# Quartered first chunk, reordered first tile, and the V tiles moved behind the QK tiles in a differential-attention and ternary-MLP kernel

## The chip, the cores and the metric

The kernel runs on one NeuronCore of a Trainium2 chip (trn2). The metric is the time of one execution on the device in microseconds (us). Engines: PE is TensorE (matrix products and transposes), DVE is VectorE, ACT is ScalarE, POOL is GpSimd, SP is SyncE, which issues nearly all the DMAs. "SPq" and "ACTq" in rows are DMA issues by SP and ACT.

## The reference, cut to what matters

One pre-norm transformer layer on `x` of shape (8, 1024, 512), float32. The head of the kernel, which the change edits, computes the normalised rows and their products with `w_qkv`.

```python
h = layernorm(x)                          # eps 1e-5, no weight
qkv = h @ w_qkv                           # (8, 1024, 1536)
q, k, v = split(qkv, 3)                   # 16 heads of 32; each head in halves of 16
a = softmax(q1 @ k1.T * s) - lam * softmax(q2 @ k2.T * s)
out = rms_norm(a @ v) * norm_w * 0.2      # then heads folded back into rows
x = x + fold(out) @ wo
h = layernorm(x)
r = relu(bitlinear(h, w_fc) + gate * (h @ v_.T @ fast_b.T @ u.T))
x = x + bitlinear(r * r, w_proj)          # ternary weights, hidden 2048
```

Products are made at near float32 accuracy from a high and a low part of both operands: `hi*hi + hi_x*lo_w + lo_x*hi_w`.

## The kernel before

**Chunks.** The 8192 rows of x are 16 chunks of 512 rows (two for each of the 8 batches, C = 0 to 15). A chunk is loaded into `xin` (128 partitions, 4 quarters `st` of 128 rows, 512 columns), normalised in place, turned by 16 PE transposes of 128x128 and split into `xhi(C)` (ACT) and `xlo(C)` (DVE).

**Tiles.** From a chunk, 12 tiles of 512 columns follow, each of 12 matmuls (4 parts `k` of the inner dimension, 3 products `part`). Indices 0 to 7 are query and key tiles (called QK tiles below) and 8 to 11 are value tiles (V tiles). `ORDER` says in which order they come; `kind_of(T)` gives chunk and index of tile T, and chunk 0 uses `ORDER[0]`, chunk 1 `ORDER[2]`. For a QK tile ACT copies PSUM to a staging slot, DVE makes the low half and the row maximum (`dve_low`, `dve_bound`), and SP stores it to DRAM as two DMAs of 256 KB. For a V tile ACT alone copies it into `vsg[V % 2]` (two slots; V = 7 goes to `stg`), and SP stores it as one DMA. ACT waits before V >= 2 until the store of V - 2 has landed (`act_tile`).

**The prologue.** 24 tiles (T = 0 to 23) of batch 0 are made ahead of the attention, in PSUM banks T % 4. Interleaved at fixed places are the LayerNorm of the next chunk (`dve_ln_step`, steps 0 to 3 statistics, 4 gather, 6 Newton, 7 to 10 apply), its turns (after tiles 6 to 9 of chunk 0, 5 to 8 of chunk 1: `FIRST_TURN`), ternary weights of the MLP (`UNIT_AT`, ACT and DVE), and the "flag" for the largest score (`dve_flag`, `pe_flag`, then `sync_shift`, four small DMAs from `mh` that ACT issues). SP goes through one fixed list: the stores in the order of T, the loads of x chunks behind T = 10 and T = 22, the loads of queries and keys for the first head pair behind T = 15, of its values behind T = 16 and at the end.

**Into the attention.** `pe_score(e, 0, 0, 0)` is the first score. It waits for the shift DMAs of `sync_shift` and for `s_ql >= 16` and `s_v >= 8`, that is for ACT to have copied the last V tile. From there 64 head pairs run, each with 3 more tiles of later chunks, then the MLP.

**The first chunk before.** One DMA of 1 MB loads it; DVE does the whole LayerNorm; then `pe_turn` turns it by column parts `k` (four transposes each, over all quarters), ACT copies the four parts after its four weight copies `wqh`, and DVE alternates `wql` part k and `xlo` part k. Tile 0 follows k by k, three products at a time, each k waiting for its `wql` and its `xlo`.

Of the kernel before, what the change touches and what calls it, by code (L numbers as in the profile page):

```python
# [33 lines left out]

TILE_BANK = (6, 7, 6)
ORDER = ((0, 1, 8, 2, 3, 9, 4, 5, 10, 6, 7, 11), (0, 1, 8, 2, 3, 9, 4, 5, 6, 7, 10, 11),
         (0, 1, 8, 2, 3, 4, 5, 6, 7, 9, 10, 11))

STG = 8

# [61 lines left out]
def build(nc, x, wqkv, wo, lq1, lq2, lk1, lk2, norm_w, fast_b, w_fc, w_proj, u, v, gate, out):  # L102
# [10 lines left out]
    with ExitStack() as top:  # L113
# [146 lines left out]
        sb2 = (sb2a, sb2b)  # L260


        s_small, s_x, s_wo, s_xr, s_x2 = (sem(n) for n in ("s_small", "s_x", "s_wo", "s_xr", "s_x2"))
        s_nw = sem("s_nw")
        s_w = [sem(f"s_w{k}") for k in range(4)]
# [213 lines left out]
                .then_inc(s_pap, 1)  # L479

        def sync_x(e, C):
            if C:
                e.wait_ge(s_xt, 4 * C)
            e.dma_start(xin[:], x_chunk(C)).then_inc(s_x, 16)

        def sync_part(e, P):

# [185 lines left out]
            e.dma_start(out_rows[rows:rows + 128, :], fo[:, rt, :]).then_inc(s_out[rt], 16)  # L673

        def sync_program(e):
            sync_x(e, 0)
            for k in range(4):
                e.dma_start(wst[:, k, :], wqk[:, k, :]).then_inc(s_w[k], 16)
            e.dma_start(gatec, gate.partition_broadcast(128)).then_inc(s_small, 16)
# [80 lines left out]
        def pe_turn(e, C, k, bk):  # L760
# [2 lines left out]
                t = e.transpose(ps[:, bk, st * 128:(st + 1) * 128], xin[:, st, k * 128:(k + 1) * 128], ident[:])  # L763
            t.then_inc(s_xt, 1)

        def pe_part(e, P):

            C, st = part_of(P)
            e.wait_ge(s_pap, P + 1)
            e.wait_ge(s_pt, 2 * P + 1)  # L770
            for k in range(4):
                t = e.transpose(ps[:, 4, k * 128:(k + 1) * 128], xin[:, st, k * 128:(k + 1) * 128], ident[:])  # L772
            t.then_inc(s_xt, 1)
# [9 lines left out]
        def pe_tile(e, T, bk, n0, n1):  # L783

            C, i = kind_of(T)
            if n0 == 0 and T == 2:
                e.wait_ge(s_wl, 8)
            for n in range(n0, n1):
                k, part = divmod(n, 3)
                if T == 0 and part == 0:  # L790
                    e.wait_ge(s_wl, k + 1)
                if i == 0 and part == 0 and C < 3:
                    e.wait_ge(s_xtl, 4 * C + k + 1)
                elif i == 0 and n == 0:
                    e.wait_ge(s_xtl, 4 * C + 4)
                w = (wqh, wql, wqh)[part]
                xx = (xhi(C), xhi(C), xlo(C))[part]
                if i < 8:
                    m0 = TILES[i] * 128
                    t = e.matmul(ps[:, bk, :], w[:, k, m0:m0 + 128], xx[:, k, :], start=(n == 0), stop=(n == 11))  # L800
                else:
                    st = i - 8
                    t = e.matmul(ps[:, bk, :], xx[:, k, st * 128:(st + 1) * 128], w[:, k, 2 * E:3 * E],  # L803
                                 start=(n == 0), stop=(n == 11))
            if n1 == 12:
                t.then_inc(s_tile, 1)
# [284 lines left out]

        def tensor_program(e):
            e.wait_ge(s_pool, 7)
            for k in range(4):
                pe_turn(e, 0, k, k)
            for T in range(24):
                C, i = divmod(T, 12)
                if T >= 4:
                    tile_read(e, T - 4)
                else:  # L1100
                    e.wait_ge(s_xtl, T + 1)

                if T == 21:
                    pe_tile(e, T, T % 4, 0, 10)
                    pe_flag(e, 0)
                    pe_tile(e, T, T % 4, 10, 12)
                else:
                    pe_tile(e, T, T % 4, 0, 12)
                k = i - FIRST_TURN[C]
                if 0 <= k < 4:  # L1110
                    if C:
                        e.wait_ge(s_xtl, 4 * C + k + 1)
                    pe_turn(e, C + 1, k, 4 + k)
# [109 lines left out]
        def act_turn(e, C, k, bk):  # L1223
            e.wait_ge(s_xt, 4 * C + k + 1)
            if C >= 2 and k == 0:
                e.wait_ge(s_tile, 12 * (C - 1))
            e.activation(xhi(C)[:, k, :], ps[:, bk, :], ACT.Copy).then_inc(s_xth, 1)

        def act_part_ln(e, w):
            e.wait_ge(s_pnv, 8 * w + 5)  # L1230
# [154 lines left out]
        def scalar_program(e):  # L1385
            e.preload_act_table_set("natural_log_exp_and_others")
            e.wait_ge(s_pool, 4)
            act_ln(e, 0, mv, ln_t, rs)
            for k in range(4):
                e.wait_ge(s_w[k], 16)  # L1390
                e.activation(wqh[:, k, :], wst[:, k, :], ACT.Copy).then_inc(s_wh, 1)
            for k in range(4):
                act_turn(e, 0, k, k)
            for T in range(24):
                C, i = divmod(T, 12)
                act_tile(e, T, T % 4)
                if T == 3:
                    e.wait_ge(s_lamv, 4)
                    e.activation(dt_[:, 2:4], dt_[:, 0:2], ACT.Exp).then_inc(s_lame, 1)
                if i == FIRST_TURN[C] - 2:  # L1400
                    act_ln(e, C + 1, mv, ln_t, rs)
                k = i - FIRST_TURN[C]
                if 0 <= k < 4:
                    act_turn(e, C + 1, k, 4 + k)
                if T == 21:

                    sync_shift(e, 0)
                if T in UNIT_AT:
                    act_magnitudes(e, UNIT_AT.index(T))
                if T - 2 in UNIT_AT:  # L1410
                    act_ternary(e, UNIT_AT.index(T - 2))
                if T == 22:
                    e.wait_ge(s_wo, 16)
                    for r in range(2):
                        e.wait_ge(s_tna[r], 16)
                    e.activation(woh[:], wos, ACT.Copy).then_inc(s_woh, 1)
# [102 lines left out]
        def dve_ln_step(e, C, n):  # L1519
# [1 line left out]
            att, f = C < 3, C - 1  # L1521
            xi, xo = (xin, xin) if att else (x2[(f + 1) % 3], xn)
            st_, mv_, ln_, rs_ = (st6, mv, ln_t, rs) if att else (st62, mv2, ln2, rs2)
            if n == 0:
                if att:
                    e.wait_ge(s_x, 16 * (C + 1))
                else:
                    e.wait_ge(s_x2l[(f + 1) % 3], 16 * (f // 3 + 1))
            if n < 4:
# [10 lines left out]
        def dve_turn(e, C, k, bk):  # L1540
            e.wait_ge(s_xth, 4 * C + k + 1)
            e.tensor_tensor(xlo(C)[:, k, :], ps[:, bk, :], xhi(C)[:, k, :], ALU.subtract).then_inc(s_xtl, 1)  # L1542

        def dve_part_stats(e, P):

            C, st = P // 4 + 3, P % 4
            for n in range(P - 1, P) if P else range(-4, 0):

                if n < 0:
                    e.wait_ge(s_x, 16 * 4)  # L1550
                else:
                    e.wait_ge(s_xp[n % 4], 16 * (n // 4 + 1))
                e.bn_stats(st6[:, n % 4, :], xin[:, n % 4, :]).then_inc(s_pst, 1)
# [209 lines left out]
        def vector_program(e):  # L1763
# [7 lines left out]
            for k in range(4):  # L1771
                e.wait_ge(s_wh, k + 1)
                e.tensor_tensor(wql[:, k, 0:2 * E], wst[:, k, 0:2 * E], wqh[:, k, 0:2 * E], ALU.subtract).then_inc(s_wl, 1)
                dve_turn(e, 0, k, k)
            for k in range(4):
                e.tensor_tensor(wql[:, k, 2 * E:3 * E], wst[:, k, 2 * E:3 * E], wqh[:, k, 2 * E:3 * E], ALU.subtract) \
                    .then_inc(s_wl, 1)
            for T in range(24):
# [16 lines left out]
                    e.wait_ge(s_nw, 16 * 4)  # L1795
                    e.tensor_scalar(nw[:], nw[:], 1.0 - LAMBDA_INIT, None, ALU.mult).then_inc(s_lamv, 1)
                k = i - FIRST_TURN[C]
                for n in ((0, 1, 2), (3, 4), range(6, 11))[k + 3] if -3 <= k < 0 else ():
                    dve_ln_step(e, C + 1, n)
                if T - 1 in UNIT_AT:  # L1800
                    dve_ternary(e, UNIT_AT.index(T - 1))
                if T == 20:
                    dve_flag(e, 0, 0)
                if 0 <= k < 4:
                    dve_turn(e, C + 1, k, 4 + k)
                if T == 21:
                    dve_flag(e, 0, 1)
                    flag = load_flag(e, 0)
                    dve_shift(e, flag, 0)
# [165 lines left out]
```

## Time and profile before

| what | value |
|---|---|
| time before, median of 3 runs | 3751.72 us (3751.03 to 3753.09) |
| the profiled execution | 3749.25 us, its span 3747.5 us |
| PE busy | 3704.4 us, 99% of the span |
| DVE / ACT / POOL busy | 84% / 75% / 17% of the span |
| first matmul of tile 0 / first score | 16.61 us / 100.83 us |
| mean granted TensorE clock | 0.998 |

The span runs from the first to the last instruction; the execution's own time is 1.75 us longer. Times in rows are us from the span's start. A timeline row gives start, duration of the whole group, engine, line, operation, output<-inputs, count and, in brackets, idle time before it and what ended it.

### The profile page before, as it was taken

To read this page: it belongs to the slowest core of one execution; us is meant where nothing else is said; L and a number is where in the kernel's file an instruction comes from. 1 tells how busy PE (TensorE), PEld (TensorE's weight loads), DVE (VectorE), ACT (ScalarE), POOL (GpSimd) and SP (SyncE) were. 2 spreads that over 40 slices of the span, in tenths; PEclk is the share of its full clock that TensorE was granted. 3 is DMA by queue.
4 is the path that set the end of the run, shared out by engine and by line. 5 is a ranking of instruction groups with operands and counts; after the bars stand their busy time and mean duration, and the time that the engine had idled before them with its cause. 6 is when DMAs were issued, how large, how long until landed. Compare 5 with 4: busy or idle time off the path is not lost.

```text
span 3747.5 us, 57714 instructions
## 1 busy us (share of the span) xinstructions
PE 3704.4 (99%) x21736; PEld 2051.2 (55%) x21736; DVE 3153.3 (84%) x2918; ACT 2795.3 (75%) x3626; POOL 622.9 (17%) x281
## 2 busy tenths in 40 slices
PE   7999999999999999999999999999999999999999
PEld 6344444444444444444444444444468888888887
DVE  6899999999999999999999999988875555555554
ACT  4788888888888888888888888889873333333333
POOL 0101001023434343223222301320020000000000
PEclk9999999999999999999999999999999999999999
DMA  7544444445444544554555444544340101010010
GB/s 246 125 104 101 105 105 105 106 99 110 101 101 101 111 106 96 112 113 104 113 110 117 98 99 103 120 100 115 78 152 23 45 23 45 23 45 23 29 40 23
DMA packets 255351, 344.58 MB, mean 92 GB/s; under 512 B 118000, under 2 KB 142576, under 8 KB 254000
## 3 DMA queue, kind: packets, MB, share of 16 engines
q1 hardware_dynamic: 251504, 324.43, 36.8%
q0 software_dynamic: 3392, 15.73, 1.4%
q8 instruction: 208, 3.41, 0.4%
q14 instruction: 119, 0.97, 0.1%
q10 hardware_dynamic: 128, 0.03, 0.0%
HBM read 198.55 MB, written 131.07 MB: 88 GB/s over the span
## 4 chain that ended last, share of the span: by engine, by line
PE 89%; DVE 7%; issue 2%; ACT 1%; DMA 0%; DVEq 0%; ACTq 0%; SPq 0%
PE ps L887 22%; PE ps L862 16%; PE ps L956 13%; PE ps L1014 12%; PE ps L800 9%; DVE acc L1652 5%; PE ps L942 5%; PE ps L803 4%; PE ps L910 3%; PE ps L961 2%; PE ps L772 1%; PE ps L1050 1%; ACT pr L1282 1%; PE ps L923 1%; PE ps L1035 1%
## 5 line engine op out<-in xcount | busy, mean ns | idle before, releaser
L1282 ACT ACTIVATE pr<-ps 128x1024 f32<-128x1024 f32 x2048 | 1990.4, 1029 | 257.6 <-PE ps L862 251.0
L1652 DVE TENSOR_TENSOR acc<-acc,pr 128x2048 f32<-128x2048 f32 x768 | 1780.7, 2319 | 41.1 <-ACT pr L1282 11.7
L887 PE MATMUL ps<-pr,vst 128*32 128x512 f32 x8192 | 1011.2, 600 | 0.0
L862 PE MATMUL ps<-qst,kst 50*128 50x512 f32 x4096 | 781.9, 456 | 9.9 <-ACT pr L1282 7.5
L862 PEld LDWEIGHTS ps<-qst,kst 50*128 50x128 f32 x4096 | 337.2, 184 | 658.8 <-ACT pr L1282 463.7
L887 PEld LDWEIGHTS ps<-pr,vst 128*32 128x32 f32 x8192 | 213.3, 109 | 446.6 <-issue 433.5
L1451 ACT ACTIVATE rb<-ps,scf 128x512 f32<-128x512 f32 x228 | 157.0, 689 | 350.5 <-PE ps L961 350.5
L1014 PE MATMUL ps<-tP,hh_ 128*128 128x512 f32 x1024 | 399.6, 390 | 1.4 <-DVE hl_ L1873 1.4
L1014 PE MATMUL ps<-tP,hl_ 128*128 128x512 f32 x1024 | 398.8, 389 | 0.0
L800 PE MATMUL ps<-xt,wqh 128*128 128x512 f32 x1024 | 376.8, 419 | 3.0 <-DVE xt L1542 3.0
L478 POOL TENSOR_SCALAR xin<-xin,mv,rs 128x512 f32<-128x512 f32 x60 | 205.7, 3432 | 876.5 <-DVE rs L1571 876.5
L956 PE MATMUL ps<-yh,tT 128*128 128x512 f32 x896 | 351.1, 392 | 0.0
L956 PE MATMUL ps<-yl,tT 128*128 128x512 f32 x896 | 348.9, 389 | 0.0
L1652 DVE TENSOR_TENSOR acc<-pr 128x2048 f32<-128x2048 f32 x128 | 294.3, 2299 | 53.3 <-ACT pr L1282 51.2
L800 PEld LDWEIGHTS ps<-xt,wqh 128*128 128x128 f32 x1024 | 189.5, 189 | 120.3 <-issue 81.9
L1014 PEld LDWEIGHTS ps<-tP,hh_ 128*128 128x128 f32 x1024 | 192.2, 188 | 43.8 <-DVE hl_ L1873 2.6
L1014 PEld LDWEIGHTS ps<-tP,hl_ 128*128 128x128 f32 x1024 | 192.2, 188 | 40.1 <-issue 0.2
L800 PE MATMUL ps<-xt,wql 128*128 128x512 f32 x512 | 202.8, 396 | 0.0
L1868 DVE TENSOR_TENSOR sb2a<-rb 128x512 f32<-128x512 f32 x114 | 78.8, 691 | 137.3 <-ACT rb L1451 137.3
L803 PE MATMUL ps<-wqh,xt 128*128 128x512 f32 x512 | 189.7, 416 | 0.0
L956 PEld LDWEIGHTS ps<-yl,tT 128*128 128x128 f32 x896 | 168.2, 188 | 34.3
L956 PEld LDWEIGHTS ps<-yh,tT 128*128 128x128 f32 x896 | 168.2, 188 | 34.1
(179 smaller groups left out, 3822.8 us busy)
## 6 DMA issues: line engine op xcount, KB each, us to landing
qst<-q_scratch SPq DMA_DIRECT2D x128, 256.0 KB, 4.7
kst<-k_scratch SPq DMA_DIRECT2D x128, 256.0 KB, 7.1
q_scratch<-stg SPq DMA_DIRECT2D x112, 256.0 KB
k_scratch<-stg SPq DMA_DIRECT2D x112, 256.0 KB
qst<-q_scratch SPq DMA_DIRECT2D x128, 128.0 KB, 5.0
kst<-k_scratch SPq DMA_DIRECT2D x128, 128.0 KB, 7.8
vst<-v_scratch SPq DMA_DIRECT2D x128, 128.0 KB, 4.7
xr<-in_L_attn_x_dram SPq DMA_DIRECT2D x64, 256.0 KB
```

Of the source, the lines that this page charges most:

```text
L478: e.tensor_scalar(xin[:, st, :], xin[:, st, :], mv[:, st, 0:1], rs[:, 8 + st:9 + st], ALU.subtract, ALU.mult) \
L800: t = e.matmul(ps[:, bk, :], w[:, k, m0:m0 + 128], xx[:, k, :], start=(n == 0), stop=(n == 11))
L803: t = e.matmul(ps[:, bk, :], xx[:, k, st * 128:(st + 1) * 128], w[:, k, 2 * E:3 * E], start=(n == 0), stop=(n == 11))
L862: ins = e.matmul(ps[:, 2 * c + hh, :], kst[rows, r, j, t * 128:(t + 1) * 128], qst[rows, r, j, c * 512:(c + 1) * 512], start=True, stop=True)
L887: ins = e.matmul(ps[32 * c4:32 * c4 + 32, 4 + j, :], vst[:, r, t, 32 * hh:32 * hh + 32], pr[:, sl, c, hh, :], start=(t == 0), stop=(t == 7 ...
L910: t = e.matmul(ps[32 * c4:32 * c4 + 32, sum_bank(X, j), :], ones[:], acc[:, j, (2 * c + hh) * 512:(2 * c + hh + 1) * 512], start=True, sto ...
L942: t = e.matmul(ps[:, 7, :], o_[:, kk, :], w_[:, kk, :], start=(kk == 0 and i == 0), stop=(kk == 3 and i == 2))
L956: t = e.matmul(ps[:, bk, :], tT[:, i, m // 2, :], (hi, lo)[m % 2][:, m // 2, :], start=(m == 0), stop=False)
L1014: t = e.matmul(ps[:, rt, :], h_[:, uu % 3, rt * 128:(rt + 1) * 128], tP[:, i, :], start=(i == 0 and part == 0), stop=(i == 15 and part == 1))
L1282: e.activation(pr[:, sl, c, :, :], ps[:, 2 * c:2 * c + 2, :], ACT.Exp, scale=SCALE).then_inc(s_exp, 1)
L1451: e.activation(rb[:, uu % 2, :], ps[:, 4 + uu % 2, :], ACT.Relu, scale=scf[:, 0, i:i + 1]) \
L1652: e.tensor_tensor(acc[:, j, :], old, new, ALU.add).then_inc(s_add, 1)
```

## The change

- The first chunk is loaded by four DMAs of 256 KB, one for each quarter of rows, each with a semaphore of its own; statistics of a quarter wait only for that quarter. `s_x` therefore counts one load less everywhere.
- It is turned by quarters: `pe_first_turn` makes the four transposes of a quarter as soon as that quarter is normalised; `act_first_turn` and `dve_first_turn` split a quarter over all column parts. ACT does this between its second and third weight copy, DVE behind its second `wql`.
- Tile 0 makes its four `hi*hi` products first, then the four with `xlo`, then the four with `wql`.
- In chunk 1 all eight QK tiles come first and the four V tiles last (T = 20 to 23; before, T = 14 and 21 to 23). The flag and the shift DMAs move one tile earlier, and the LayerNorm steps of chunk 2 are moved forward by one tile (statistics and gather behind T = 14, Newton and apply behind T = 15).

```diff
@@ -34,7 +34,7 @@
...
 ORDER = ((0, 1, 8, 2, 3, 9, 4, 5, 10, 6, 7, 11), (0, 1, 8, 2, 3, 9, 4, 5, 6, 7, 10, 11),
-         (0, 1, 8, 2, 3, 4, 5, 6, 7, 9, 10, 11))
+         (0, 1, 2, 3, 4, 5, 6, 7, 8, 9, 10, 11))
 
@@ -260,6 +260,7 @@
...
 
+        s_x0 = [sem(f"s_x0{k}") for k in range(4)]
         s_small, s_x, s_wo, s_xr, s_x2 = (sem(n) for n in ("s_small", "s_x", "s_wo", "s_xr", "s_x2"))
@@ -479,9 +480,12 @@
...
         def sync_x(e, C):
-            if C:
-                e.wait_ge(s_xt, 4 * C)
+            e.wait_ge(s_xt, 4 * C)
             e.dma_start(xin[:], x_chunk(C)).then_inc(s_x, 16)
+
+        def sync_first_x(e):
+            for st in range(4):
+                e.dma_start(xin[:, st, :], x_chunk(0)[:, st, :]).then_inc(s_x0[st], 16)
 
@@ -673,7 +677,7 @@
...
         def sync_program(e):
-            sync_x(e, 0)
+            sync_first_x(e)
             for k in range(4):
@@ -763,6 +767,12 @@
...
 
+        def pe_first_turn(e, st):
+            e.wait_ge(s_lnv, 13 + st)
+            for k in range(4):
+                t = e.transpose(ps[:, st, k * 128:(k + 1) * 128], xin[:, st, k * 128:(k + 1) * 128], ident[:])
+            t.then_inc(s_xt, 1)
+
         def pe_part(e, P):
@@ -787,11 +797,19 @@
...
                 k, part = divmod(n, 3)
-                if T == 0 and part == 0:
-                    e.wait_ge(s_wl, k + 1)
-                if i == 0 and part == 0 and C < 3:
+                if T == 0:
+                    k, part = (n % 4, 0) if n < 4 else (n % 4, 2) if n < 8 else (n % 4, 1)
+                    if part == 0:
+                        e.wait_ge(s_wh, k + 1)
+                    if part == 1:
+                        e.wait_ge(s_wl, k + 1)
+                if T == 0 and n == 0:
+                    e.wait_ge(s_xth, 4)
+                if T == 0 and n == 4:
+                    e.wait_ge(s_xtl, 4)
+                if i == 0 and part == 0 and 0 < C < 3:
                     e.wait_ge(s_xtl, 4 * C + k + 1)
-                elif i == 0 and n == 0:
+                elif C and i == 0 and n == 0:
                     e.wait_ge(s_xtl, 4 * C + 4)
@@ -1091,8 +1109,8 @@
...
             e.wait_ge(s_pool, 7)
-            for k in range(4):
-                pe_turn(e, 0, k, k)
+            for st in range(4):
+                pe_first_turn(e, st)
             for T in range(24):
@@ -1100,7 +1118,7 @@
...
 
-                if T == 21:
+                if T == 20:
                     pe_tile(e, T, T % 4, 0, 10)
@@ -1226,6 +1244,11 @@
...
 
+        def act_first_turn(e, st):
+            e.wait_ge(s_xt, st + 1)
+            e.activation(xhi(0)[:, :, st * 128:(st + 1) * 128], ps[:, st, :].rearrange("p (k n) -> p k n", k=4), ACT.Copy) \
+                .then_inc(s_xth, 1)
+
         def act_part_ln(e, w):
@@ -1387,10 +1410,11 @@
...
             for k in range(4):
+                if k == 2:
+                    for st in range(4):
+                        act_first_turn(e, st)
                 e.wait_ge(s_w[k], 16)
                 e.activation(wqh[:, k, :], wst[:, k, :], ACT.Copy).then_inc(s_wh, 1)
-            for k in range(4):
-                act_turn(e, 0, k, k)
             for T in range(24):
@@ -1402,7 +1426,7 @@
...
                     act_turn(e, C + 1, k, 4 + k)
-                if T == 21:
+                if T == 20:
 
@@ -1521,9 +1545,11 @@
...
             st_, mv_, ln_, rs_ = (st6, mv, ln_t, rs) if att else (st62, mv2, ln2, rs2)
-            if n == 0:
+            if C == 0 and n < 4:
+                e.wait_ge(s_x0[n], 16)
+            if n == 0 and C:
                 if att:
-                    e.wait_ge(s_x, 16 * (C + 1))
+                    e.wait_ge(s_x, 16 * C)
                 else:
@@ -1541,13 +1567,19 @@
...
 
+        def dve_first_turn(e, st):
+            e.wait_ge(s_xth, st + 1)
+            cols = slice(st * 128, (st + 1) * 128)
+            e.tensor_tensor(xlo(0)[:, :, cols], ps[:, st, :].rearrange("p (k n) -> p k n", k=4), xhi(0)[:, :, cols],
+                            ALU.subtract).then_inc(s_xtl, 1)
+
         def dve_part_stats(e, P):
...
                 if n < 0:
-                    e.wait_ge(s_x, 16 * 4)
+                    e.wait_ge(s_x, 16 * 3)
                 else:
@@ -1771,7 +1803,9 @@
...
                 e.tensor_tensor(wql[:, k, 0:2 * E], wst[:, k, 0:2 * E], wqh[:, k, 0:2 * E], ALU.subtract).then_inc(s_wl, 1)
-                dve_turn(e, 0, k, k)
+                if k == 1:
+                    for st in range(4):
+                        dve_first_turn(e, st)
             for k in range(4):
@@ -1795,15 +1829,16 @@
...
                 k = i - FIRST_TURN[C]
-                for n in ((0, 1, 2), (3, 4), range(6, 11))[k + 3] if -3 <= k < 0 else ():
+                steps = ((range(5), range(6, 11), ()) if C else ((0, 1, 2), (3, 4), range(6, 11)))
+                for n in steps[k + 3] if -3 <= k < 0 else ():
                     dve_ln_step(e, C + 1, n)
...
                     dve_ternary(e, UNIT_AT.index(T - 1))
-                if T == 20:
+                if T == 19:
                     dve_flag(e, 0, 0)
...
                     dve_turn(e, C + 1, k, 4 + k)
-                if T == 21:
+                if T == 20:
                     dve_flag(e, 0, 1)
```

## Rows read from the trace of the kernel before

**Rows 1.** The page: busy times of the engines.

```profile
PE 3704.4 (99%) x21736; PEld 2051.2 (55%) x21736; DVE 3153.3 (84%) x2918; ACT 2795.3 (75%) x3626; POOL 622.9 (17%) x281
```

**Rows 2.** Timeline, 0 to 23 us: first chunk, weights and tile 0.

```profile
6.23 2.47 DVE L1494 BATCH_NORM_STATS2 st<-xin 128x6 f32<-128x512 f32 x4 [5.13 <-DMA xin<-in_L_attn_x_dram]
...
9.52 5.74 ACT L1391 ACTIVATE wqh<-wst 128x1536 fp32r<-128x1536 f32 x4
...
12.15 1.22 DVE L1773 TENSOR_TENSOR wql<-wst,wqh 128x1024 fp32r<-128x1024 f32 x1
...
12.38 3.65 PE L763 MATMUL ps<-ident,xin 128*128 128x128 f32 x16 [12.38 <-DVE xin L1516]
15.16 2.04 ACT L1227 ACTIVATE xt<-ps 128x512 fp32r<-128x512 f32 x4
...
22.36 0.62 PE L800 MATMUL ps<-xt,wqh 128*128 128x512 f32 x2
```

**Rows 3.** DMA issues of 1.35 to 1.8 and 3.1 to 3.4 us: KB, us to landing.

```profile
wst<-in_L_attn_w_qkv_dram SPq DMA_DIRECT2D x1, 768.0 KB, 6.7
...
wst<-in_L_attn_w_qkv_dram SPq DMA_DIRECT2D x1, 768.0 KB, 10.7
```

**Rows 4.** Windows of 2 us: stretch, length, each engine's busy us (instructions), PEclk, DMA share, GB/s.

```profile
92.00:94.00 2.00, 2.00 (x17) 1.66 (x17) 1.06 (x5) 0.60 (x1) 0.00 (x0) 1.00 0.52 196
...
98.00:100.00 2.00, 0.46 (x3) 0.04 (x1) 0.64 (x1) 1.81 (x2) 0.00 (x0) 1.00 0.83 267
100.00:102.00 2.00, 0.73 (x4) 0.33 (x4) 1.65 (x1) 0.64 (x1) 0.00 (x0) 1.00 0.55 208
102.00:104.00 2.00, 1.56 (x4) 1.03 (x5) 0.00 (x0) 2.00 (x3) 0.00 (x0) 0.50 0.78 257
```

**Rows 5.** Timeline, 66 to 80 us: the LayerNorm of chunk 2.

```profile
66.40 1.67 DVE L1729 TENSOR_SCALAR wf<-wf,scf 128x512 f32<-128x512 f32 x4
...
75.74 1.91 DVE L1516 TENSOR_SCALAR xin<-xin,mv,rs 128x512 f32<-128x512 f32 x4
...
77.80 1.09 PE L763 MATMUL ps<-ident,xin 128*128 128x128 f32 x4 [5.79 <-DVE xin L1516]
...
79.54 1.05 PE L800 MATMUL ps<-xt,wqh 128*128 128x512 f32 x2
```

**Rows 6.** Timeline of PE and ACT, 89 to 118 us: last copies, first scores.

```profile
89.18 0.60 PE L763 MATMUL ps<-ident,xin 128*128 128x128 f32 x4
...
94.18 2.65 ACTq L568 DMA_DIRECT2D qst<-mh  x4
96.93 0.60 ACT L1265 ACTIVATE vsg<-ps 128x512 f32<-128x512 f32 x1 [3.29 <-issue]
...
99.23 0.59 ACT L1265 ACTIVATE stg<-ps 128x512 f32<-128x512 f32 x1
...
100.83 0.73 PE L862 MATMUL ps<-qst,kst 50*128 50x512 f32 x4 [2.36 <-DMA qst<-mh]
...
117.15 1.92 PE L887 MATMUL ps<-pr,vst 128*32 128x512 f32 x16
```

**Rows 7.** Timeline of SP's DMA issues, 96 to 106 us.

```profile
96.53 4.65 SPq L515 DMA_DIRECT2D v_scratch<-vsg  x2
101.23 4.84 SPq L484 DMA_DIRECT2D xin<-in_L_attn_x_dram  x1
```

**Rows 8.** SP's own waits, 0 to 110 us: us in total, times, longest.

```profile
SPq L498 <- DVE stp L1586: 16.4, 6, 7.1
```

**Rows 9.** V stores issued at 28.86, 96.53, 97.79, 135.05 us: us to landing.

```profile
v_scratch<-vsg SPq DMA_DIRECT2D x1, 256.0 KB, 5.4
...
v_scratch<-vsg SPq DMA_DIRECT2D x1, 256.0 KB, 10.5
...
v_scratch<-vsg SPq DMA_DIRECT2D x1, 256.0 KB, 10.1
...
v_scratch<-vsg SPq DMA_DIRECT2D x1, 256.0 KB, 3.0
```

## The prediction

> **What bounds the kernel now.** I began with the page: PE is busy 99% of the span [rows 1]. From the first score at 100.83 us on, the kernel is a full PE, and nothing there is edited. So the change is worth what it moves the first score by, and I read only the first 107 us. The timeline of that stretch shows three places where PE is not full: tile 0, fed piece by piece, so that tile 1 starts only at 22.36 + 0.23 = 22.59 us [rows 2]; a hole of 5.79 us ahead of the first turn of chunk 2 [rows 5]; and 2.36 us ahead of the first score, which waits for the shift DMAs [rows 6]. The change aims at all three. Then I read the list of SP's issues and the landings of its V stores, because the change puts the V tiles last, and a V copy on ACT waits for an older V store.
>
> **1. The first chunk and tile 0: a gain of 2.4 us.** The statistics start at 6.23, when the whole megabyte has landed [rows 2]. With quarters the last is issued some 1.5 us later than now's one issue and lands by 6.2 at the latest (the megabyte's landing now), so that the LayerNorm ends at least 1.9 us sooner: three of its four statistics (0.6 each) are done before. The first turn starts behind the first apply instead of the fourth. That would put the 16 turns (3.65 us) at about 8.5 to 12.1. The three extra issues, 1.5 us on SP, stand ahead of the weight loads; I cost them at nothing, since these land 6.7 to 10.7 us after their issue, queued behind one another [rows 3]; without that cover they cost 1.5.
>
> The end is set by the weights. The first and the last of the four, issued at 1.3 and 3.0, land at 1.3 + 6.7 = 8.0 and 3.0 + 10.7 = 13.7 [rows 3], and the two between at about 9.9 and 11.8. ACT: weight copies of 1.43 each (5.74 for four) at 8.0 and 9.9, to 11.35; four splits of 0.51 (2.04 for four) to 13.4; two more weight copies to 14.85 and 16.3. DVE: the second `wql` at 11.35 to 12.55, four `xlo` splits of 0.61 to 15.0, the third `wql` to 16.2, the fourth at 16.3 to 17.5 [rows 2]. PE: `hi*hi` products at 13.5 (two), 14.9 and 16.35, then eight products that wait for nothing but the last `wql`. At 0.23 us a product tile 1 starts at 18.4, a gain of 4.2; at the lower clock's 0.42 (1.05 less 0.63 for the second of a pair, [rows 5]) it starts at 16.35 + 9 x 0.42 = 20.15, a gain of 2.4. Which? Between 98 and 102 PE was busy 1.19 of 4 us, and the granted clock then read 0.50, which is 1.2 GHz [rows 4]. Between 12.1 and 16.3 PE would hold three products, about 1.2 us of 4.2. That is nearly the same, so I take 2.4 and keep 4.2 as the other end. If the weight loads do lose their 1.5 us, the gain is 0.9, which is the low end.
>
> **2. LayerNorm of chunk 2 one tile earlier: 1.9 us, which nothing will use.** The statistics stand between the work of tiles 14 and 15, and the apply, behind tile 16, starts at 75.74 [rows 5]. In the new order tile 14 is a QK tile, so DVE first makes its low half and maximum (from the end of the ternary work at 66.40 + 1.67 = 68.1, at 0.6 each, to 69.3), then four statistics of 0.6 (a quarter of 2.47, [rows 2]) and the gather of 0.4, to 72.1, tile 15's two to 73.3, Newton's four small steps of 0.65 in all, and the apply at 73.95. 75.74 - 73.95 is 1.8; with rounding 1.9. PE's hole shrinks from 5.79 to 3.9 us, still long enough for the low clock. It costs nothing else: the same instructions in another order. PE then finishes tile 23 earlier, but see 4.
>
> **3. Flag and shift one tile earlier: 1.7 us, likewise unused.** The last turn now begins at 89.18, the shift DMAs at 94.18 and the score at 100.83, 11.65 after that turn [rows 6]. Moved up, the DMAs go out about 3.7 after that turn (ACT's copy of tile 20 and its turn, DVE's turn, the flag, and the same 1.0 us to the issue), and behind them on ACT stand 2.65 us of issuing, then three V copies and `woh` (0.5, 0.5, 1.8, 0.6): the last V copy ends 9.8 after the turn. That is what the score would wait for, if nothing else were late.
>
> **4. V tiles last: a new wait, which decides.** V copy number 6 (T = 22) waits for the store of V number 4. Before, number 4 was T = 14, some 22 us older; now it is T = 20, two tiles older. So when does T = 20's store land? SP's list is late: it spends 4.65 us on issuing two V stores, and these land 10.5 and 10.1 us after issue [rows 7, 9], at 107.0 and 107.9. T = 20's new store has ahead of it all that T = 21's had, less one V store (that of T = 14), and one V store is worth 107.9 - 107.0 = 0.9. It also inherits the gain of 2.4 from the head, because SP does catch up with the compute early on: it waited 16.4 us for DVE's low halves in all [rows 8]. So it lands at 107.0 - 0.9 - 2.4 = 103.7. Behind it on ACT stand that V copy, `woh` and the last V copy: from 96.93 to 99.23 + 0.59 = 99.82 in [rows 6], 2.9 us, with 0.15 for the hand-overs 3.05. The score needs `s_v` of 8, so it starts at 106.75. PE ends tile 23 at 100.83 - 2.36 = 98.5 today, with the gains of 1 and 2 at about 94, and then stands idle for over 12 us.
>
> That is 106.75 - 100.83 = 5.9 us later than now. Behind the waiting copy also stand SP's entries for V 6, x chunk 3, V 7 and the first pair's second half of values. The x load takes 4.84 to issue [rows 7], so V 7's store lands at about 103.7 + 0.6 + 4.8 + 5.4 (a landing at half load, [rows 9]) = 114.5, and its reload with another 3 comes at 117.5; its reader is the fifth step of value products, now 16.3 us after the first score (117.15, [rows 6]), so at 123. It is covered by 5 us.
>
> The one case for headroom is the DMA share: 0.52 at 92 to 94 us [rows 4], as if half of the capacity were free, with which the store would land in 5.4 (the first, at half load) or 3.0 us (a quiet stretch) [rows 9]. Against it is the 10.5 in the same stretch, and I go by that. The Trainium skill ("DMA: Bandwidth & Descriptors", section "Why a DMA increments its semaphore by 16 and not by 1") says that a DMA is spread over the largest number up to 16 of engines that divides the outermost dimension of both sides. A QK store's DRAM side has 8 heads outermost, so by that rule it fills eight engines and leaves eight idle, and a V store, which needs all 16, lands behind that queue. The rule and the 10.5 agree and give +5.9; without the rule the share would give about +0.8. No row here tells the engines apart.
>
> **Sum.** The profiled execution took 3749.25; 3749.25 + 5.9 = 3755.15. It lies 2.47 under the median of the three runs, so in terms of that median I predict 3751.72 + 5.9 = 3757.6, 0.16% slower. About 0.2% (7.5 us) is what a measurement of this kernel can tell from no change: below 3744.2 is faster, above 3759.2 slower.
>
> **The rivals.**
> - *The V store lands soon (15%).* Its issue at 96.53 - 0.9 - 2.4 = 93.2 and 5.4 or 3.0 to landing give 98.6 or 96.2, the score at 101.65 or 99.25: +0.8 or -1.6, so 3752.5 to 3750.1. For it speaks the share of 0.52, against it all landings near 10.
> - *The change does all it aims at (9%).* The wait never binds: 2.4 + 1.9 + 1.7 = 6.0 earlier, 3745.7; with the high clock in tile 0 another 1.8, 3743.9. For it: on paper each of the three holes gets smaller. Against it: V number 4 would have to land within about 7 us of T = 20's end, on a queue where it isn't even issued by then.
> - *SP's backlog, not the compute, sets the store (10%), slower.* If the queue is never drained between chunk 0 and T = 20, the head's gain doesn't reach it, and T = 20's store is issued no earlier than T = 21's today: landing 107.0, score at 110.05, +9.2, 3760.9. It decides once SP is behind by more than 2.4 us throughout. For it: two issues that take 4.65 us. Against: SP's 16.4 us of waiting for DVE.
> - *The forecast (66%).* With the high clock in tile 0 it is 3755.8, with only 0.9 of gain 3759.1, and a landing 2 us off either way moves it as much: 3753.5 to 3760 is its own range.
>
> **How the numbers follow.** Predicted is the likeliest, 3757.6. The range must leave out no more than 2 in 10: 3748.5 to 3760.5 takes in the forecast and the soon landing (81%) and leaves out both ends. Faster by over 0.2% is only the second rival with the high clock and some luck: 6%. Slower is the third rival and the top of the forecast's own range: 10 + 6 = 16%. Within 0.2%: 78%.
>
> **What would show it.** Right: ACT's V copy of T = 22 idle for 6 us or more ahead of it, with the store of T = 20 as its end; first score near 106 to 107; PE idle for 12 us or more before it instead of 2.36; tile 1 starting between 18 and 20.5 us; PE's hole ahead of chunk 2's turn near 3.9. Wrong at step 1: tile 1 starts after 21.5. Wrong at step 4: the V copy of T = 22 starts within 1 us of its tile, and the score waits for the shift DMAs again. The prediction as a whole fails if the V store lands much off 10 us after its issue, or if the first pairs, from 100 to 160 us, take longer or shorter than now.

## The result and the profile after

| | before | after |
|---|---|---|
| median | 3751.31 us (17 runs, 3748.08 to 3754.71) | 3759.30 us (17 runs, 3753.45 to 3762.99) |
| profiled execution, its span | 3749.25, 3747.5 us | 3760.06, 3758.0 us |
| first score | 100.83 us | 111.08 us |
| from the first score to the end of the span | 3646.7 us | 3646.9 us |

After takes 1.0022 times as long as before (95% interval 1.0015 to 1.0028): 8.0 us more in the medians, where 5.9 were predicted. The whole difference of the two spans, 10.5 us, is there by the first score (+10.25). I read the page first:

```profile
PE 3705.1 (99%) x21736; PEld 2052.1 (55%) x21736; DVE 3153.7 (84%) x2918; ACT 2794.2 (74%) x3626; POOL 628.6 (17%) x281
```

Beside [rows 1] PE, DVE and ACT work as long as before to within 1.1 us (POOL 5.7 longer), so the added time is idle time. Where it stands, the waits of after between 24 and 130 us say (engine, line, what ended them: us in total, times, longest):

```profile
PE ps L880 <- ACT stg L1288: 16.2, 1, 16.2
ACT vsg L1288 <- DMA v_scratch<-vsg: 14.4, 1, 14.4
```

One wait of ACT and one of PE behind it. The timelines of ACT, PE and SP from 84 to 113 us, which answer to [rows 6, 7]:

```profile
86.26 0.60 ACT L1288 ACTIVATE vsg<-ps 128x512 f32<-128x512 f32 x1 [2.58 <-PE ps L821]
...
90.27 2.70 ACTq L572 DMA_DIRECT2D qst<-mh  x4
93.06 0.60 ACT L1288 ACTIVATE vsg<-ps 128x512 f32<-128x512 f32 x1 [5.72 <-PE ps L821]
108.06 0.60 ACT L1288 ACTIVATE vsg<-ps 128x512 f32<-128x512 f32 x1 [14.39 <-DMA v_scratch<-vsg]
108.55 1.90 ACT L1440 ACTIVATE woh<-acc 128x2048 fp32r<-128x2048 f32 x1
110.35 0.59 ACT L1288 ACTIVATE stg<-ps 128x512 f32<-128x512 f32 x1
```

```profile
111.08 1.22 PE L880 MATMUL ps<-qst,kst 50*128 50x512 f32 x4 [16.23 <-ACT stg L1288]
```

```profile
89.91 5.02 SPq L509 DMA_DIRECT2D q_scratch<-stp  x2
95.03 1.82 SPq L509 DMA_DIRECT2D k_scratch<-stp  x2
96.90 2.15 SPq L519 DMA_DIRECT2D v_scratch<-vsg  x1
```

T = 20's tile is copied at 86.26, but SP issues its store only at 96.90, since the stores of the two QK tiles ahead of it (89.91 and 95.03 above, two DMAs each) take 6.8 us to issue. The store's own row (KB, us to landing) answers to [rows 9]:

```profile
v_scratch<-vsg SPq DMA_DIRECT2D x1, 256.0 KB, 11.1
```

It lands at 108.0. Only then may ACT copy T = 22 (108.06); `woh` and the last V copy follow, and PE scores at 111.08, 3.1 us after the landing. The shift DMAs, for which PE waited before, were issued at 90.27, 3.9 us sooner than in [rows 6].

The head, 3 to 21 us, which answers to [rows 2]:

```profile
3.54 1.29 DVE L1518 BATCH_NORM_STATS2 st<-xin 128x6 f32<-128x512 f32 x2 [2.44 <-DMA xin<-in_L_attn_x_dram]
...
7.06 0.69 DVE L1518 BATCH_NORM_STATS2 st<-xin 128x6 f32<-128x512 f32 x1 [0.47 <-DMA xin<-in_L_attn_x_dram]
...
10.07 3.49 PE L773 MATMUL ps<-ident,xin 128*128 128x128 f32 x16 [10.07 <-DVE xin L1540]
...
17.06 2.50 PE L818 MATMUL ps<-xt,wqh 128*128 128x512 f32 x5 [0.87 <-ACT wqh L1417]
...
19.36 1.43 PE L818 MATMUL ps<-xt,wql 128*128 128x512 f32 x4
...
20.62 0.39 PE L818 MATMUL ps<-xt,wqh 128*128 128x512 f32 x1
```

The last quarter of x is read at 7.06, later than the whole megabyte before (6.23). From 17.06 to 19.36 five of tile 0's products pass, 0.46 us apiece, and the granted clock from 18 to 20 us reads 0.50, the low one (1.2 GHz); the last four come 0.32 apart, across its return to the high one, and tile 1 starts at 20.62, 1.97 us sooner than before's 22.59. PE's hole ahead of chunk 2's turn, against 5.79 in [rows 5]:

```profile
74.37 0.77 PE L767 MATMUL ps<-ident,xin 128*128 128x128 f32 x4 [4.31 <-DVE xin L1540]
```

### The profile page after: what moved, and what is told of

Same layout as the page of the kernel before. It is cut to its first block, busy times and chain, and to the rows that moved or that the text cites. A ratio compares the mean times of both kernels' runs of the same rounds, so it can differ in the third digit from the quotient of the medians.

```text
span 3758.0 us, 57714 instructions
## 1 busy us (share of the span) xinstructions
PE 3705.1 (99%) x21736; PEld 2052.1 (55%) x21736; DVE 3153.7 (84%) x2918; ACT 2794.2 (74%) x3626; POOL 628.6 (17%) x281
## 4 chain that ended last, share of the span: by engine, by line
PE 87%; DVE 7%; issue 2%; ACT 2%; DMA 1%; SPq 1%; DVEq 0%; ACTq 0%
PE ps L905 22%; PE ps L880 16%; PE ps L974 13%; PE ps L1032 12%; PE ps L818 8%; DVE acc L1684 6%; PE ps L960 5%; PE ps L821 4%; PE ps L928 3%; PE ps L979 2%; PE ps L782 1%; PE ps L1068 1%; ACT pr L1305 1%; PE ps L1053 1%; PE ps L941 1%
```

## The experiments

Each was timed in five rounds against before (its median lay at 3750.1 to 3750.8). Scores and holes are read from one profiled execution each, and single executions of one kernel spread by some 3 to 10 us in time. "Old layout" and "new layout" refer to the scratch in DRAM; the four kernels whose names begin with k16 have the new one.

| kernel | median us (runs) | ratio to before, 95% | first score us | PE idle before it |
|---|---|---|---|---|
| head_only | 3749.44 (11) | 0.9997, 0.9988 to 1.0006 | 98.83 | 2.55 for the shift DMAs |
| head_ln | 3746.49 (11) | 0.9993, 0.9984 to 1.0002 | 97.83 | 3.27 for the shift DMAs |
| order_only | 3761.74 (8) | 1.0026, 1.0016 to 1.0037 | 113.39 | 14.69 for ACT's last V copy |
| v6_slot | 3749.32 (11) | 0.9996, 0.9987 to 1.0005 | 98.99 | 1.78 for the shift DMAs |
| v4_act | 3750.53 (11) | 1.0001, 0.9992 to 1.0010 | 106.53 | 10.55 for ACT's last V copy |
| head_ln_defer | 3746.29 (11) | 0.9990, 0.9981 to 0.9999 | 98.37 | 3.36 for the shift DMAs |
| k16_before | 3744.51 (11) | 0.9987, 0.9978 to 0.9996 | 100.50 | 1.35 for ACT's last V copy |
| k16_head_ln | 3740.06 (8) | 0.9972, 0.9962 to 0.9983 | 96.92 | 1.35 for ACT's last V copy |
| k16 | 3739.13 (10) | 0.9973, 0.9963 to 0.9982 | 95.41 | 1.11 for ACT's last V copy |
| k16_v6 | 3740.52 (11) | 0.9976, 0.9967 to 0.9985 | 95.70 | 1.02 for ACT's last V copy |

### The parts of the change by themselves

head_only is after with the old order, flag and LayerNorm places; head_ln keeps the new LayerNorm places as well; order_only is before with the new order, flag and LayerNorm places and the old head.

```diff
-         (0, 1, 2, 3, 4, 5, 6, 7, 8, 9, 10, 11))
+         (0, 1, 8, 2, 3, 4, 5, 6, 7, 9, 10, 11))   # head_only, head_ln; flag and shift at T = 20, 21
...
-                steps = ((range(5), range(6, 11), ()) if C else ((0, 1, 2), (3, 4), range(6, 11)))
+                steps = ((0, 1, 2), (3, 4), range(6, 11))   # head_only
```

> The changed kernel with only its first part: quartered first chunk and tile 0; order of chunk 1, flag and LayerNorm steps as before. Theory (the copy of V number 6 waits for the store of V number 4): no wait for a V store, first score 0.8 to 2.2 us earlier than before (99 to 100), ratio 0.9994 to 1.0. Rival (the loss sits in the head: a lower clock in tile 0, later weights): first score later than before, ratio above 1.001.

> As the run with the first part alone, and the LayerNorm of chunk 2 one tile earlier; order and flag as before, so V number 4 stays at T = 14. Theory: the hole ahead of chunk 2's turn shrinks by 1.9 us and, with no V wait to swallow it, the first score comes 2.7 to 4.1 us earlier than before; ratio 0.9989 to 0.9993. Rival (SP's backlog delays the load of chunk 2, so the earlier place gains nothing): same as the first part alone.

> The kernel before with only the second part: QK tiles first in chunk 1, flag and LayerNorm of chunk 2 one tile earlier; the first chunk as before. Theory with SP's backlog setting the store of T = 20: issued at 96.5 to 98, landing near 108, first score near 111, +10 us, no more than in the changed kernel. Theory with the compute setting it: everything 2.2 us later than in the changed kernel, first score 113.3, +12.5. Rival (the loss needs the new head): at most +1.

head_only and head_ln have no wait on a V store, and their first score comes 2.0 and 3.0 us sooner than before. Their medians are 1.4 and 4.3 us lower, within what the measurement can tell from no change. order_only has the whole loss and more: 3761.74, with SP issuing T = 20's store at 99.85 and ACT standing 13.5 us for it (SP's row, then ACT's).

```profile
99.85 11.49 SPq L515 DMA_DIRECT2D v_scratch<-vsg  x3
```

```profile
110.36 0.60 ACT L1265 ACTIVATE vsg<-ps 128x512 f32<-128x512 f32 x1 [13.52 <-DMA v_scratch<-vsg]
```

So the loss belongs to the second part (order, flag and LayerNorm places), and the head gives back a little of it. Of the two theories that order_only was to tell apart, its first score (113.39, +12.6) is the one of the compute setting the store (113.3, +12.5), and its issue at 99.85 lies outside the 96.5 to 98 of SP's backlog setting it. It is one execution; what it weighs against the others is taken up below.

### The wait taken away by a slot

v6_slot is after with V number 6 copied to `stg[0]`, which no other tile of the prologue uses, so that ACT has no V store to wait for.

```diff
-            return stg[:, 1, 0, :].bitcast(F32) if V == 7 else vsg[:, V % 2, :]
+            return stg[:, V - 6, 0, :].bitcast(F32) if V in (6, 7) else vsg[:, V % 2, :]
...
-                if V >= 2 and V != 7:
+                if V >= 2 and V not in (6, 7):
```

> The changed kernel, with V number 6 staged in the free query slot stg[0] instead of vsg[0], so that its copy waits for no store. Theory: the 14.4 us wait of ACT is gone; ACT's last V copy ends near 96, the shift DMAs land near 96.8, first score near 97, 14 us earlier than in the changed kernel and 4 earlier than before. Not all of it may last: the values' second half is reloaded only when V number 7's store has landed, near 115, and its reader comes 16.3 us after the score, near 113.5; if so, 3 to 5 us come back there, and the ratio is 0.9995 to 1.0005; if not, 0.9989. Rival (PE's low clock or the head makes the loss, the wait only covers it): first score falls by less than 5 us.

The first score comes 12.1 us sooner than in after, at 98.99, and the median is 10 us lower. SP issues T = 20's store no earlier (97.09), so it is the wait, not the store, that cost the time. The score comes 2 us later than the 97 I had expected, since it waits for the shift DMAs. In the first pair ACT stands 3.0 us, and not where I had looked for it: its exponentials write where QK tiles are still waiting to be stored. The profiled execution pays 1.0 us behind the first score (3647.9 us to the end, against 3646.9 in after); that these waits are the reason isn't shown.

```profile
102.31 1.02 ACT L1305 ACTIVATE pr<-ps 128x1024 f32<-128x1024 f32 x1 [0.83 <-DMA k_scratch<-stp]
...
107.45 2.94 ACT L1305 ACTIVATE pr<-ps 128x1024 f32<-128x1024 f32 x3 [2.20 <-DMA k_scratch<-stp]
```

### SP's queue, or the DMA engines?

Two theories explain a store that is late. Either SP reaches it late, and then another issuer helps; or the engines are full, and then only less work for them does. v4_act lets ACT issue T = 20's store, ahead of its shift DMAs.

```diff
             for T in range(24):
-                sync_store(e, T)
+                if T != 20:
+                    sync_store(e, T)
...
                 if T == 20:
+                    sync_store(e, T)
                     sync_shift(e, 0)
```

> The changed kernel, with one DMA moved: the store of T = 20 (V number 4) is issued by ACT ahead of the shift DMAs instead of by SP. Theory (V number 4 lands late because it stands behind the QK stores on SP's queue): issued near 88, it lands well before T = 22's copy is due or a few us behind it, as the shift DMAs on ACT's queue land 2.6 to 4.5 us after issue; the 14.4 us wait falls below 3; first score near 98 to 100; ratio 0.9985 to 1.0005 to the kernel before. Rival (the DMA engines themselves are full, whichever queue is used): it lands near 100 or later, the wait stays above 6 us.

```profile
88.02 0.43 ACTq L519 DMA_DIRECT2D v_scratch<-vsg  x1
91.29 2.54 ACTq L572 DMA_DIRECT2D qst<-mh  x4
93.93 0.60 ACT L1289 ACTIVATE vsg<-ps 128x512 f32<-128x512 f32 x1 [5.46 <-PE ps L822]
103.50 0.60 ACT L1289 ACTIVATE vsg<-ps 128x512 f32<-128x512 f32 x1 [8.98 <-DMA v_scratch<-vsg]
```

```profile
90.00:92.00 2.00, 2.00 (x11) 1.65 (x10) 0.00 (x0) 0.00 (x0) 0.00 (x0) 1.00 1.05 177
```

Issued 8.9 us sooner than in after, the store landed 15.4 us after its issue, at 103.4, only 4.6 us sooner. The engines' share was 0.97 or more in each window of 2 us from 88 to 98 us (one is shown: the last two columns are the DMA share and GB/s), so the rival holds: about half of the lead was lost on full engines, although the store had a queue of its own. The first score moved by as much (106.53). The median, 3750.53, can't be told from before's any more; the profiled execution, 3754.14, is one of the slowest of its 11, and SP was later in it than in after (T = 19's store at 98.66 against 95.03), so the 4.6 us are rough.

head_ln_defer asks the same of SP's list in head_ln: the last two ternary stores go out in the first pair instead.

```diff
-                if T - 2 in UNIT_AT:
+                if T - 2 in UNIT_AT[0:2]:
                     sync_ternary(e, UNIT_AT.index(T - 2))
...
+                    if P == 0 and d in (1, 3):
+                        sync_ternary(e, 2 + d // 3)
```

> First part and earlier LayerNorm, order and flag as before, and the last two of the four ternary stores (512 KB each) are issued in the first head pair instead of behind T = 13 and 14. Theory (the queue is the backlog): all that SP issues after them goes out 2 to 3 us earlier and the shift DMAs land 1 to 2 us earlier: first score 96 to 97, ratio 0.9985 to 0.9992. Rival (the shift chain is set by the flag's compute): first score stays at 97.8 within 0.5.

The V store of T = 21 was issued at 93.45 instead of 96.56, and PE waited 3.36 us for the shift DMAs as before: 3746.29 against head_ln's 3746.49, no gain.

### What fills the engines: the layout of the QK scratch

A QK store wrote to a scratch whose outermost dimension is the 8 heads. k16 is after with the part outermost, so that the 8 heads and 16 rows of a part merge into 128 rows of one stride; the loads then need twelve DMAs per head pair instead of eight, of the same bytes. k16_before is before, k16_head_ln is head_ln and k16_v6 is v6_slot with the same layout. The waits for a pair's loads, which the cut leaves out, count 192 instead of 128.

```diff
-    qsc = nc.dram_tensor("q_scratch", [2, 4, 8, 2, 16, S], F32, kind="Internal").ap()
+    qsc = nc.dram_tensor("q_scratch", [2, 4, 2, 8, 16, S], F32, kind="Internal").ap()
...
-                e.dma_start(sc[:, part, :, c * 512:(c + 1) * 512], stage(Q)[:, part, :].bitcast(F32)) \
+                e.dma_start(sc[part].rearrange("g d s -> (g d) s")[:, c * 512:(c + 1) * 512], stage(Q)[:, part, :].bitcast(F32)) \
...
-                    rows = sc[b % 2, tile, s0 + 2 * hh:s0 + 2 * hh + 2]
+                    rows = sc[b % 2, tile, :, s0 + 2 * hh:s0 + 2 * hh + 2]
+                    for r0, part in ((64 * hh + both, 0), (64 * hh + both + 16, 1), (64 * hh + again, 0)):
+                        e.dma_start(dst[r0:r0 + 16, r, :, :].bitcast(F32), rows[part].rearrange("j d s -> d j s")) \
...
```

> The changed kernel with the scratch of queries and keys laid out with its high and low part outermost, so that a QK store writes 128 rows in one stride instead of 8 groups of 16; each pair's queries and keys then need 12 loads instead of 8. Theory (the QK stores fill only half of the DMA engines and so make SP's queue late): a QK store's stretch shows a share near 1 and about 400 GB/s instead of 0.52 and 200, the store of T = 20 is issued 5 us or more earlier (92 or earlier) and the wait for it shrinks by as much or more; first score at or below 106. Rival (the share of 0.5 is the cost of writing to DRAM, not of the layout): share and rate stay, the store still lands near 108. In both cases the 4 extra issues of each pair may cost something later.

> The same layout with the first part and the earlier LayerNorm, but order and flag as before. Theory: queue and V wait are both out of the way; the load of chunk 2 lands earlier, the shift DMAs land sooner behind the emptier engines; first score 1 to 4 us earlier than with the old layout (97.8); ratio 0.9980 to 0.9992. Rival: the extra loads of each pair cost more than this gives; ratio above 0.9995.

> The kernel before with nothing but the new layout of the query and key scratch (a store of 128 rows in one stride, twelve loads per head pair). Theory (the half-filled DMA engines are what makes SP and its stores late): the first score was waiting for the shift DMAs 2.36 us, behind that for nothing; with the queue drained the shift DMAs land in about 2 us, so the first score comes 2 to 5 us sooner than before's 100.83, and the rest of the gain of the layout (the runs with layout and new head were 10 to 11 us under before, the head alone 1.4 to 4) comes from the tiles' stores in the first stretch: 3742 to 3745 us in all against 3750. Rival (the layout's gain belongs to the whole run of 64 head pairs, whose loads are twelve instead of eight and whose stores are shorter): the first score comes within 1 us of 100.83, but the time still falls by 6 us or more.

> The kernel after with the new layout of the query and key scratch and with V number 6 staged in its own slot. Theory: with the stores on time V number 4 has landed before ACT wants its slot (no wait in the run with the layout alone), so the slot of its own adds nothing: 3739 us within 0.05%. Rival (the copy still waits a little at places that the layout only shortened): 1 to 2 us sooner, 3737.5.

Windows in which a QK store is what is under way (0.5 us; the last two columns are the DMA share and GB/s), of after and then of k16:

```profile
51.00:51.50 0.50, 0.50 (x4) 0.42 (x3) 0.00 (x0) 0.50 (x3) 0.00 (x0) 1.00 0.53 201
```

```profile
50.00:50.50 0.50, 0.50 (x3) 0.39 (x3) 0.00 (x0) 0.50 (x3) 0.00 (x0) 1.00 1.02 389
```

In after the QK store used half of the engines' time at 201 GB/s, as the 0.52 of [rows 4] had; with 128 rows outermost the share is 1.02 and the rate 389. k16 also changes the loads of queries and keys, so those have to be looked at too. Windows of 2 us with these loads under way, after and then k16:

```profile
88.00:90.00 2.00, 2.00 (x11) 1.65 (x10) 0.74 (x5) 0.00 (x0) 0.00 (x0) 1.00 1.06 131
```

```profile
78.00:80.00 2.00, 2.00 (x12) 1.65 (x11) 0.52 (x1) 1.09 (x2) 0.00 (x0) 1.00 1.04 131
```

They fill the engines at 131 GB/s in both layouts, and take about as long to land (medians of 5.7 us for the queries and 7.4 and 9.0 for the keys in after, of 4.6 and 8.0 in k16), so it is the stores' rate that the layout changed. In after these loads, issued from 79.18 to 86.58, are a second thing that keeps the engines full ahead of T = 20's store. SP's own waits from 50 to 97 us show what the stores' rate does to its list: in after it hardly waits (4.1 us), because it is behind; in k16 it waits for 27 of the 47 us. First after, then the longest of k16:

```profile
SPq L509 <- ACT stp L1283: 1.8, 2, 1.3
SPq L580 <- ACT tt L1370: 1.5, 1, 1.5
SPq L502 <- DVE stp L1618: 0.8, 1, 0.8
```

```profile
SPq L502 <- DVE stp L1616: 10.4, 7, 2.3
SPq L519 <- ACT vsg L1286: 7.8, 2, 5.8
SPq L578 <- ACT tt L1368: 7.0, 4, 3.2
```

In k16 the store of T = 20 is issued at 86.33 (the first of SP's row, whose length takes in waits for the copies of T = 21 and 22) and lands 5.4 us later, and the copies of T = 21 and 22 (the first row of ACT below) follow their tiles and wait for no store:

```profile
86.33 7.69 SPq L519 DMA_DIRECT2D v_scratch<-vsg  x3
```

```profile
91.89 1.09 ACT L1286 ACTIVATE vsg<-ps 128x512 f32<-128x512 f32 x2 [5.09 <-PE ps L819]
...
95.94 2.85 ACT L1303 ACTIVATE pr<-ps 128x1024 f32<-128x1024 f32 x3 [0.68 <-PE ps L878]
```

With the layout in both, the change does what it aims at: the first score moves from 100.50 (k16_before) to 95.41 (k16), the medians from 3744.51 to 3739.13 (no run of k16 is above 3741.50, none of k16_before below 3743.51). The order part is no loss there: k16 against k16_head_ln is 1.5 us sooner at the first score and 0.9 us in the medians, which isn't told apart from nothing. k16_v6 gains nothing over k16; the slot is not needed once the store is on time. k16 has the lowest median of all: 0.27% under before, 0.54% under after (3739.13 to 3759.30).

On k16_before the theory failed, and its rival came near. The first score is 0.3 us sooner, not 2 to 5, since ACT's last V copy ends at 100.4 anyway; yet it takes 5.6 us less. From the first score to the end the eight profiled kernels with the old layout take 3643.6 to 3647.9 us and the four with the new one 3641.2 to 3643.4, so some 3 to 4 us of the layout's gain lie in the head pairs. Two differences are on record there. PE's waits for DVE's sums (`acc`) from 117 to 3745 us are 3.8 to 4.3 us in the eight and 2.2 to 2.8 in the four. And the granted clock is 0.50 for 6.5 to 11.4 us behind the first score in the eight, for 3.4 to 6.8 in the four. How the layout brings either about isn't shown.

## Why the prediction was right, and where it was off

**Step 1, the head: size nearly right, one bound wrong.** Predicted 2.4 us with tile 0 at the low clock, measured 1.97 (tile 1 at 20.62 where I had 20.15), 2.0 in head_only (20.57). The bound "lands by 6.2 at the latest" failed: the last quarter was there at 7.06. Three statistics were done by then, so the LayerNorm still gained, but half of it: the apply starts at 9.38 instead of 10.32, 0.94 sooner instead of the 1.9 I gave at least. The cover of the three extra issues was only partly there: the first weights were ready for ACT at 8.95 where I had 8.0, the second at 10.83 where I had 9.9, so some 0.9 of the 1.5 us came through. About half of that was made good behind: the last `wqh` copy ended at 17.0 instead of 16.3, and the products after it ran partly at the high clock, so tile 1 came 0.47 late.

**Step 2, the LayerNorm of chunk 2: right.** Hole 4.31, predicted 3.9 (1.5 us of the 1.9), and nothing used it.

**Step 3, flag and shift: right, with the issue somewhat late.** The shift DMAs were issued 3.9 us sooner than before and 4.2 after the last turn, where I had 3.7; nothing used that either. What the score would wait for with the V store on time, k16 shows: ACT's last V copy, which ends at 95.27, 9.8 us after the last turn (85.51), as I had it. In v6_slot it waited 1.78 us for the shift DMAs instead. Steps 1 to 3 together, 6.0 us on paper, gave 5.1 at the first score with the new layout (100.50 to 95.41).

**Step 4, the new wait: right in kind, one term mis-sized.** T = 20's store is the end of ACT's wait, the score waits for ACT's last V copy, and from landing to score there are 3.1 us as I had it. The term that failed is the issue of that store, "107.0 - 0.9 - 2.4": I had it at 93.2, and it was at 96.90; the landing took 11.1 instead of 10.5. So the score came at 111.08 instead of 106.75. The 3.7 us are found in SP's list. Its ternary store behind T = 13, at 69.18 in before, should have moved up by 2.4 and was at 69.63, so 2.85 of them were lost by then, and from there to the V store it gained 0.1 instead of 0.9. The two DMAs of T = 13 and the ternary store, before and after:

```profile
65.93 3.20 SPq L505 DMA_DIRECT2D k_scratch<-stp  x2
69.18 1.52 SPq L576 DMA_DIRECT2D t_scratch<-tt  x1
```

```profile
64.96 4.62 SPq L509 DMA_DIRECT2D k_scratch<-stp  x2
69.63 0.52 SPq L580 DMA_DIRECT2D t_scratch<-tt  x1
```

The 0.9 shows in no profiled kernel: from that ternary store to the V store SP took 27.35, 27.87 and 27.71 us in the old order (before, head_only, head_ln; T = 21's store) and 27.27, 28.05 and 29.06 in the new one (after, v6_slot, order_only; T = 20's). Nor does the head's gain get there reliably. In the five profiled kernels with the new head, the old layout and that store at its place, which run the same program up to it, it was issued at 66.69 (head_only), 68.85 (head_ln), 69.04 (v6_slot), 69.63 (after) and 72.16 (v4_act): 2.5 us sooner to 3.0 later than in before, though tile 1 started 1.5 to 2.3 us sooner in all of them. With the new layout the gain does get there: against k16_before, tile 1 started 2.43, 2.11 and 1.47 us sooner (k16, k16_v6, k16_head_ln), and this store was issued 2.48, 2.10 and 1.32 sooner. So this is the place where my argument for the head's gain broke. SP's 16.4 us of waiting for DVE [rows 8] lie early, 14.2 of them before 50 us; from 50 to 97 us it waits for compute 4.6 us in before and 4.1 in after, and its issues lengthen.

Whether the backlog alone set T = 20's store, as the third rival had it (landing 107.0, score at 110.05, +9.2; I gave it 10%), stays open. The profiled +10.25 is nearer to it than to the forecast's +5.9. Against it stands order_only: with the old head that store was issued 2.95 us later than in after (99.85 to 96.90), as if the head's gain had come through whole. But v4_act, with the new head, came to T = 19's store at 98.66, later than order_only (97.83), so single executions differ by more than what is to be told apart.

**Why the median is still near.** The profiled execution of after is 0.8 us above its median and that of before 2.1 below, so of their 10.8 us of difference the medians show 8.0. Predicted was 3757.6, measured 3759.30; the range 3748.5 to 3760.5 holds it. That it came so near is in part luck: at the first score the forecast was 4.3 us short. "Within 0.2%", given 78%, isn't settled: 3759.30 lies just above the 3759.2 that I had named, and the interval, 1.0015 to 1.0028, has 1.002 inside.

**The reason behind the landing of 10.5 us.** I had leaned on the Trainium skill ("DMA: Bandwidth & Descriptors", section "Why a DMA increments its semaphore by 16 and not by 1"): a DMA is spread over the largest number of engines up to 16 that divides the outermost dimension of both sides. k16 bears it out: with 128 rows instead of 8 heads outermost the share of a QK store goes from 0.53 to 1.02 and the rate from 201 to 389 GB/s, and the wait of 14.4 us is gone. The rival that the store would land soon took half of the capacity for free. The rows are in keeping with a free half that is of no use to a V store, which needs the full half too; no row tells the engines apart.

**Left open.** How much the T = 14 slot's V store was worth in SP's list, since 0.1 and 0.9 us are less than the spread of SP's list between executions; whether the order itself makes SP later; and how the new layout saves its 3 to 4 us behind the first score.

## What to carry to other kernels

Before putting tiles that share a double buffer next to each other, look when the store that frees the buffer would land, and take that from the state of the queue in that very stretch, not from waits summed over a longer one. A DMA share that sits at one half while single issues last microseconds is no headroom; here it was the layout: look at the outermost dimension of the transfer first. And a gain at the head came through to SP's later issues here only where the queue ran empty in between; where it did not, one profiled execution said little about where such an issue will stand, for the same program put it up to 5.5 us apart.

## What the runs showed of the hardware

- SP's issue of a DMA isn't of fixed cost. The two DMAs of a QK store took 1.2 us to issue in the same list where those of the next took 5.0 (after, 88.62 and 89.91 us), and mostly 0.8 in k16_before, where the engines kept up.
- A store of 256 KB with 8 outermost ran at 201 GB/s with a share of 0.53 (after, 51 us), with 128 rows outermost at 389 with 1.02 (k16, 50 us). A full share isn't a full rate either: the loads of queries and keys took 1.06 of the engines' time at 131 GB/s (after, 88 to 90 us).
- Cutting a load brings its first part sooner, at 3.46 to 3.62 us instead of 6.10 to 6.23. The last of the four parts of 256 KB was read at 7.06 in after and at 6.37 in k16_v6, and within 7.0 in the others with the new head, so it comes at about the time of the whole or up to 0.8 us later.
- A store issued on ACT's queue while SP's was backed up took 15.4 us to land (v4_act, share 0.97 or more from 88 to 98 us) against 11.1 on SP's (after): a queue of its own did not bring it past full engines.
- The pace of tile 0 differs between executions of one and the same head: that of before gave its products 0.23 to 0.34 us apart in the profile of before, and 0.43 to 0.56 apart for the most part in k16_before, which has the same head. The granted clock reads 1.00 there in both, but k16_before's spacing is near the 0.46 of after, where it reads 0.50 (18 to 20 us). A forecast should keep both.
